# One squaring on the off-diagonal tiles, betas in a pass of their own, key softmax in thirds, twenty pairs per pass

## The reference

```
qkvb = (normed @ W_slow.T).reshape(slen, bsz, H, 5 * D + 2)
q, k, v, rk, rv, beta, rbeta = jnp.split(qkvb, ...)
q, k, rk = softmax(q), softmax(k), softmax(rk)
beta, rbeta = sigmoid(beta), sigmoid(rbeta)
W <- W + beta * outer(v - W k, k)   for each of the 64 rows, z = W q
```

## Time and profile before

| what | us |
|---|---|
| median of 3 runs (20809.05 to 20821.86) | 20810.57 |
| the profiled execution | 20815.45 |
| its span | 20813.7 |
| the delta stage in it, from 6423 to 12034 | 5611 |
| the recurrence behind it, from 12034 to 17085 | 5051 |

### The profile page before, as it was taken

One profiled execution on the slowest core, in us unless ns is written; L12 is line 12 of the kernel. 1 busy time (PEld: TensorE's weight loads), 2 busy tenths in 40 slices (PEclk: granted clock), 3 DMA queues, 4 the chain that ended last, 5 costly groups with the idle time before them and its releaser, 6 DMA issues. The chain is left out here.

```text
span 20813.7 us, 632597 instructions
## 1 busy us (share of the span) xinstructions
PE 14670.6 (70%) x283775; PEld 11976.0 (58%) x283775; DVE 10693.2 (51%) x24317; ACT 6016.6 (29%) x12817; POOL 2224.9 (11%) x1152
## 2 busy tenths in 40 slices
PE   4526777772666989888888966666666665767776
PEld 3414666662445777777777744555544555645554
DVE  6532455555124444444444466666667662445555
ACT  3001244440212444444444411111111111234441
POOL 0066000001460111111111100000000000000001
PEclk9555566665767999999999966777666786877785
DMA  0323200002332111111111122210122215146663
GB/s 21 92 42 70 56 16 13 8 16 77 71 58 61 21 21 20 20 21 20 21 20 21 21 41 40 40 39 17 36 40 41 41 32 153 32 138 183 178 174 76
DMA packets 1836442, 1098.30 MB, mean 53 GB/s; under 512 B 1109402, under 2 KB 1763645, under 8 KB 1816765
## 3 DMA queue, kind: packets, MB, share of 16 engines
q1 hardware_dynamic: 1606323, 999.32, 19.9%
q0 software_dynamic: 227328, 57.19, 1.9%
HBM read 569.43 MB, written 484.53 MB: 51 GB/s over the span
## 5 line engine op out<-in xcount | busy, mean ns | idle before, releaser
L2846 PE MATMUL recur_acc<-recur_U,recur_W 8*32 8x64 f32 (+4 forms) x49152 | 1389.4, 270 | 460.1 <-ACT recur_W L2770 429.3
L2897 DVE TENSOR_TENSOR recur_pr<-recur_K,recur_e 124x64 f32<-124x64 f32 (+60 forms) x1024 | 1285.3, 1255 | 648.3 <-ACT recur_e L2782 493.1
L2846 PEld LDWEIGHTS recur_acc<-recur_U,recur_W 8*32 8x32 f32 (+4 forms) x49152 | 1061.7, 140 | 869.8 <-ACT recur_W L2770 740.2
L2833 PE MATMUL recur_acc<-recur_R,recur_E 128*32 128x64 f32 x62976 | 1202.9, 232 | 187.7 <-issue 177.9
L2902 DVE TENSOR_REDUCE recur_dot<-recur_pr 124x1 f32<-124x64 f32 (+60 forms) x1024 | 1279.2, 1249 | 21.2
L2818 PE MATMUL recur_wT<-const_ident,recur_w 128*128 128x128 f32 (+15 forms) x1536 | 477.8, 373 | 1112.2 <-DVE recur_w L2904 1101.9
L2833 PEld LDWEIGHTS recur_acc<-recur_R,recur_E 128*32 128x32 f32 x62976 | 1073.1, 118 | 288.8 <-issue 230.5
L2770 ACT ACTIVATE recur_W<-recur_wT 128x256 f32<-128x256 f32 (+16 forms) x1024 | 334.8, 327 | 2603.5 <-PE recur_wT L2818 2600.5
L2475 ACT ACTIVATE delta_B0l<-delta_pS 128x512 f32<-128x512 f32 x984 | 531.8, 540 | 1687.4 <-PE delta_pS L2370 1687.4
L2475 ACT ACTIVATE delta_B1l<-delta_pS 128x512 f32<-128x512 f32 x984 | 533.1, 542 | 1407.1 <-PE delta_pS L2370 1407.1
L2818 PEld LDWEIGHTS recur_wT<-const_ident,recur_w 128*128 128x128 f32 (+15 forms) x1536 | 168.2, 143 | 1281.7 <-DVE recur_w L2904 928.2
(11 more groups left out here) (605 smaller groups left out, 34471.9 us busy)
## 6 DMA issues: line engine op xcount, KB each, us to landing
scr<-rel_BD SPq DMA_DIRECT2D x128, 1288.0 KB
rel_sc<-scr SPq DMA_DIRECT2D x128, 861.0 KB
xnT<-ln_xT SPq DMA_DIRECT2D x64, 492.0 KB, 3.0
kr<-delta_QK SPq DMA_DIRECT2D x492, 64.0 KB, 2.3
ur<-delta_Uf SPq DMA_DIRECT2D x492, 64.0 KB, 2.2
zz<-delta_Z SPq DMA_DIRECT2D x492, 64.0 KB, 2.2
recur_K<-kr SPq DMA_DIRECT2D x64, 448.0 KB
recur_H<-zz SPq DMA_DIRECT2D x64, 448.0 KB
```

Of the source, the lines that this page charges most:

```text
L2833: nc.tensor.matmul(acc[a][32 * q:32 * q + 32, 0:FD], E[a][:, EQ * q + 32 * j:EQ * q + 32 * j + 32], R[a][:, m, :], start=(j == 0), stop=False)
L2846: ins = nc.tensor.matmul(acc[a][32 * q:32 * q + 32, 0:FD], W[a][0:8 * k, b, 160 * q + 32 * j:160 * q + 32 * j + 32], U[a][0:8 * k, 2 * (t ...
L2897: V.tensor_tensor(pr[0:cp, 0:n, :], K[a][0:cp, r0:r0 + n, :], e[a][0:cp, None, :].to_broadcast([cp, n, FD]), ALU.mult).then_inc(s_own[a], 1)
```

## The change

- Matrix, transposed matrix and u of a level lie side by side in one buffer (`[128, 4, 3, 64]`). A head's product on the diagonal tiles has 128 moving columns: the transposed matrix and u together, into `pM[k]`. The other square goes from the upper partitions to the lower half of `pS[k]` and from the lower partitions to the upper half, on the two off-diagonal tiles. One semaphore (`s_S`) tells of both; `s_R` is gone.
- ScalarE copies `pS[k]` back in two instructions of 64 partitions each, crossing the halves, then waits until VectorE has read its half of the bank `pM[k]` (`s_dv`), and copies the other half of `pM[k]`.
- The betas of all pairs are computed in a step of their own ahead of the loop: 246 products of 16 columns straight from `X`, 4 sigmoids, 4 square roots. In the loop VectorE copies a pair's betas to a small buffer. 5 projections are left, in slots 0 to 4.
- Maximum, subtraction, exponential and sum are done for each of the three key kinds by itself, in slots 2 to 4, 5 to 7 and 7 to 9 (before: 5, 9 and 12). The scaling stays one instruction.
- A pass of the loop has 20 pairs in place of 6: 6 passes of 20, then the 3 left.

The core of the diff:

```diff
-        pR = [st.ps(f"pR{k}", [128, 8, FD]) for k in range(2)]
-        pS = [st.ps(f"pS{k}", [128, 4, 2, FD]) for k in range(2)]
+        pM = [st.ps(f"pM{k}", [128, 4, 2, FD]) for k in range(2)]
+        pS = [st.ps(f"pS{k}", [128, 8, FD]) for k in range(2)]
...
-        MAX_AT, EXP_AT, SUM_AT = 5, 9, 12
+        MAX_AT, EXP_AT, SUM_AT = 2, 5, 7
...
                         if SQ * G + l:
                             pe.wait_ge(s_ac[k], SQ * G + l)
+                            pe.wait_ge(s_dv[k], SQ * G + l)
+                        more = slice(1, 3) if l < SQ - 1 else slice(2, 3)
                         for a in range(4):
                             for h in HALF:
-                                ins = mm(pS[k][h, a, 0, :], now[h, a, 1, :], now[h, a, 0, :])
-                                if l < SQ - 1:
-                                    ins = mm(pS[k][h, a, 1, :], now[h, a, 0, :], now[h, a, 1, :])
+                                mm(pM[k][h, a, more.start - 1:2, :], now[h, a, 0, :], now[h, a, more, :])
+                            for x, h in enumerate(HALF):
+                                ins = mm(pS[k][HALF[1 - x], a, :], now[h, a, 1, :], now[h, a, 0, :])
                         ins.then_inc(s_S[k], 1)
-                        if SQ * G + l:
-                            pe.wait_ge(s_dv[k], SQ * G + l)
-                        for a in range(4):
-                            for h in HALF:
-                                ins = mm(pR[k][h, a, :], now[h, a, 0, :], u[h, a, :])
-                        ins.then_inc(s_R[k], 1)
...
                             act.wait_ge(s_S[k], SQ * G + l + 1)
-                            m = 2 if l < SQ - 1 else 1
-                            nc.scalar.activation(level(k, G % 2, l + 1)[0][:, :, 0:m, :], pS[k][:, :, 0:m, :], ACT.Copy).then_inc(s_ac[k], 1)
+                            new = level(k, G % 2, l + 1)
+                            for x, h in enumerate(HALF):
+                                ins = nc.scalar.activation(new[h, :, 0, :], pS[k][HALF[1 - x], 0:4, :], ACT.Copy)
+                            if l < SQ - 1:
+                                act.wait_ge(s_dv[k], SQ * G + l + 1)
+                                ins = nc.scalar.activation(new[:, :, 1, :], pM[k][:, :, 0, :], ACT.Copy)
+                            ins.then_inc(s_ac[k], 1)
...
-                        if n == EXP_AT:
-                            act.wait_ge(s_sh, p + 1)
-                            nc.scalar.activation(QK[:, 0:3, :], QK[:, 0:3, :], ACT.Exp).then_inc(s_ex, 1)
+                        if n - EXP_AT in range(3):
+                            j = n - EXP_AT
+                            act.wait_ge(s_sh, 3 * p + j + 1)
+                            nc.scalar.activation(QK[:, j, :], QK[:, j, :], ACT.Exp).then_inc(s_ex, 1)
...
-        NP, US_ = T // 2, 6
+        NP, US_ = T // 2, 20
+        banks = (gp[0][:], gp[1][:], pT[0][:].rearrange("p a d -> p (a d)"), pT[1][:].rearrange("p a d -> p (a d)"))
+        part = lambda n: slice(32 * n, min(32 * n + 32, NP))
+        with st.step() as block:
+            @block.tensor
+            def _(pe):
+                for n in range(4):
+                    for p in range(part(n).start, part(n).stop):
+                        for x, h in enumerate(HALF):
+                            ins = nc.tensor.matmul(banks[n][h, 2 * FH * (p - 32 * n):2 * FH * (p - 32 * n) + 2 * FH], X[:, :, 2 * p + x],
+                                                   W[:, 5 * KW:PROJ], start=True, stop=True)
+                    ins.then_inc(s_g, 1)
...
```

More of the change, by code:

```diff
@@ L2288, in delta_stage @@
         QK = st.sb("QK", [128, 5, KW])
-        sb_ = st.sb("sb", [128, FH, 2])
+        beta = st.sb("beta", [128, T // 2, FH, 2])
+        sb_ = [st.sb(f"sb{q}", [128, FH, 2]) for q in range(2)]
         mx = st.sb("mx", [128, 3 * FH])
@@ L2296, in delta_stage @@
         half_mask = [st.sb(f"hm{what}", [128, FD]) for what in "ULZ"]
-        pair_of = lambda what: (st.sb(f"B{what}", [128, 4, 2, FD]), st.sb(f"U{what}", [128, 4, FD]))
-        first = [[pair_of(f"{k}{g}") for g in range(2)] for k in range(2)]
-        later = [[pair_of(f"{k}l{x}") for x in range(3)] for k in range(2)]
+        first = [[st.sb(f"B{k}{g}", [128, 4, 3, FD]) for g in range(2)] for k in range(2)]
+        later = [[st.sb(f"B{k}l{x}", [128, 4, 3, FD]) for x in range(3)] for k in range(2)]
         level = lambda k, g, l: first[k][g] if l == 0 else later[k][(1, 0, 1, 2)[l - 1]]
@@ L2322, in delta_stage @@
         s_v = st.sem("values_ready")
-        s_R = [st.sem(f"applied{k}") for k in range(2)]
-        s_S = [st.sem(f"squared{k}") for k in range(2)]
+        s_S = [st.sem(f"squared_applied{k}") for k in range(2)]
         s_T = [st.sem(f"tail{k}") for k in range(2)]
@@ L2373, in head @@
                         j, g = divmod(G, 2)
-                        now, u = level(k, g, l)
+                        now = level(k, g, l)
                         if l == 0 and j:
@@ L2507, in _ @@
                     for p in range(preps):
[L2508 to L2509 removed]
+                        for j in range(3):
+                            pool.wait_ge(s_mx, 3 * p + j + 1)
+                            nc.gpsimd.tensor_tensor(third(j), third(j), mx[:, rows_of(j)].unsqueeze(2).to_broadcast([128, FH, FD]), ALU.subtract).then_inc(s_sh, 1)
                         pool.wait_ge(s_sm, p + 1)
[L2511 removed]
+                        nc.gpsimd.tensor_tensor(qk, qk, sm[:].unsqueeze(2).to_broadcast([128, 3 * FH, FD]), ALU.mult).then_inc(s_k, 1)
                 @block.vector
@@ L2644, in _ @@
                         own(nc.gpsimd.tensor_copy(half_mask[m][h, :], full[h, h]))
-        NP, US_ = T // 2, 6
+        NP, US_ = T // 2, 20
[10 more added lines that the diff above has]
+                    ins.then_inc(s_g, 1)
+            @block.scalar
+            def _(act):
+                flat = lambda n: beta[:, part(n)].rearrange("p n h a -> p (n h a)")
+                for n in range(4):
+                    act.wait_ge(s_g, n + 1)
+                    nc.scalar.activation(flat(n), banks[n][:, 0:2 * FH * (part(n).stop - part(n).start)], ACT.Sigmoid).then_inc(s_be, 1)
+                for n in range(4):
+                    act.wait_ge(s_be, n + 1)
+                    nc.scalar.activation(flat(n), flat(n), ACT.Sqrt).then_inc(s_e, 1)
+                act.wait_ge(s_e, 4)
         step_of(0, 0, 1)
```

98 lines of the change are left out of this document (48 added, 50 removed).

## The result

The changed kernel takes 19779.6 us as the median of 4 runs (19740.95 to 19799.73) against 20809.8 us: a ratio of 0.9502, 95% interval 0.949 to 0.9514. A second measurement of both kernels gave 19845.5 against 20879.3 us, 0.9502 again (0.9486 to 0.9518). The forecast was 19820 us with a range of 19500 to 20250.

What follows compares the result with a forecast made beforehand. TensorE's order of work was taken as the bound. From 20810.6 us, 701 for shorter pairs (35.5 against 41.19 us) and 325 for fewer pass ends were subtracted, 35 added for the betas' step: about 19820 us, range 19500 to 20250.

Steps and rivals of the forecast that it cites:

- What bounds it: Delta stage, inside a pair: TensorE's order of work is the bound, 31.2 us of work a pair after the change.
- Heads: TensorE's heads, tiles independent: 0.90 us at levels 0 to 2, 0.46 at level 3, saving 7.9 us a pair.
- tiles in turns: Rival: off-diagonal tiles share strips or keep program order; a head takes 1.36 us, total time 20440 us; chance 14%.
- Copies: ScalarE's copies after a head: 0.38 us each, 0.59 becomes about 1.12 us; ScalarE 23.0 us a pair against 18.4.
- the copies bind: Rival: a ScalarE copy crossing halves costs 0.594 us; a pair takes 38 us, total time 20130 us; chance 14%.
- Waits: TensorE's waits for copies, keys, masks and Z: 4.3 us a pair, bounds 1.7 (as before) to 7.
- The betas' step: One step ahead of the loop with all betas' products and activations: costs 35 us once, from 20 to 150.
- Passes: Ends of a pass, 23.2 us each: 20 become 6, saving 325 us (280 to 350).
- slower: Rival: TensorE's clock falls to 1.2 GHz for a share of the work; at 0.35, total time 21160 us; chance 6%.

Runs made afterwards that it cites:

- the version with the old heads: Changed kernel with the squares back on the diagonal tiles and one ScalarE copy, as before the change: 20321.9 us, 0.9719 of the kernel before; 39.4 us a pair.
- the version with the diagonal square: Changed kernel with the second square on the diagonal tiles too, no copy crossing halves: 20402.7 us, 0.9757 of the kernel before; 40.25 us a pair.
- The late scaling: Changed kernel with reciprocal and scaling of the softmax sums in slot 11 in place of 9: 19781.2 us, 34.8 us a pair.
- the early key: Changed kernel with ScalarE's copy of the second transposed key in slot 17, ahead of the copies of slot 18: 19786.3 us, 34.9 us a pair.
- the three moves together: Changed kernel with scaling in slot 11, second key's copy in slot 17, first two value products in slots 14 and 15: 19657.6 us, 33.9 a pair.
- the whole softmax: Changed kernel with maximum, subtraction, exponential and sum of all three key kinds in one piece again: 20140.9 us, 38.0 us a pair.
- the betas in the loop: Changed kernel with the betas' projection and table loads back in the loop, everything behind one slot later: 20357.8 us, 39.9 us a pair.

## Why the prediction was right, point by point

- **What bounds it**: right. TensorE's work is 35.35 less 3.9 of waits (the rows above and smaller ones, 479 us over 123 pairs without "issue" and the start of the loop), 31.4 us a pair; 31.2 was forecast. Part of this agreement is luck. In the version with the old heads the work is 38.7 us by the same reckoning, so the squares take away 7.3 us where 7.9 was forecast, and the betas some 0.9 where 0.4 was forecast.
- **Heads**: 0.90 us forecast, 0.88 measured. At level 3 0.46 were forecast, and 6844.05 to 6844.57 is 0.52, in a head that starts behind a wait. The tiles run independently; the version with the diagonal square shows that nothing else in the head brings it. The rival "tiles in turns" is refuted by this kernel: narrow and wide records run side by side, and the first narrow records of a head (6840.59) start before records that are issued ahead of them (6840.64 and 6840.69). The Trainium skill, "TensorE: Matmul & The Clock Gate", part 3, has matmuls start and end strictly in program order; over different tiles these rows contradict it for the starts (ends are modelled).
- **Copies**: priced right. The groups of ScalarE, as in the earlier trace rows:

```profile
L2469 ACT ACTIVATE delta_B0l<-delta_pS 64x256 f32<-64x256 f32 x1968 | 743.4, 378 | 868.5 <-PE delta_pS L2369 850.6
...
L2472 ACT ACTIVATE delta_B0l<-delta_pM 128x256 f32<-128x256 f32 x738 | 282.9, 383 | 8.6
...
L2667 ACT ACT_TABLE_LOAD x1 | 1.3, 1283 | 79.6 <-PEq L78 79.6
```

A copy takes 0.378 or 0.383 us where 0.38 was forecast, and one across the halves costs no more than another (0.378 us too in the version with the diagonal square, where nothing crosses). Three table loads are left in the whole stage, one each at L2667, L2670 and L2487 (two in the betas' step and one ahead of the first exponential), where there were three in each pair. The rival "the copies bind" falls with the price.
- **Waits**: 4.3 us a pair forecast, 3.9 measured, but not each where it was put. The stretch of slots 5 to 14 has 1.11 + 0.51 + 0.30 = 1.9 (2.2 forecast), its largest part through the very chain that was followed. The first Gram product waits 1.17 for the keys (0.8 forecast). Masks cost 0.3, Z and the projection together 0.1, where 1.3 was forecast for the three, and a wait for the first copy of a pair (0.3, delta_xc) was not foreseen.
- **The betas' step**: 35 us forecast, 34.8 measured from the stage's first transfer to the first copy (61.4 against 26.6 us). The timeline of it:

```profile
6411.02 15.03 PE L2658 MATMUL delta_gp<-delta_W,delta_X 128*64 128x16 f32 x256 [33.40 <-PEq L78]
...
6425.84 13.87 PE L2658 MATMUL delta_pT<-delta_W,delta_X 128*64 128x16 f32 x236
...
6441.59 2.12 ACT L2670 ACTIVATE delta_beta<-delta_beta 128x512 f32<-128x512 f32 x4
6445.94 0.28 DVE L2540 COPY delta_xc<-delta_X 128x128 f32<-128x128 f32 x1 [67.99 <-PEq L78]
```

The 492 records take 28.7 us (6411.02 to 6439.71): 58 ns each, twice the 29 forecast, at a clock of 0.50 throughout. In return three of the four sigmoids and a table load run beside them, where the forecast had added all eight activations and all three loads. The sum came right with two of its terms off, which is luck.
- **Passes**: 325 us forecast, 331 measured by themselves. In the changed kernel an end costs 55.76 - 35.35 = 20.4 us (19.8 on average of its six), less than before; why was not tested.
- **What the forecast had wrong** is what each edit is worth. It gave the betas 0.4 us of TensorE a pair and counted their table loads as hidden (85 us of waits, "replaced by the waits above"), and it gave the thirds nothing. In the changed kernel the betas' move is worth 4.6 us a pair and the thirds 2.6. The sum survived because it was made for the end state, in which both are gone from ScalarE's path. For the squares alone the same method (work and waits added) gave 37.5 in the expectation above, and 40.8 was measured: it left out that long or close waits also lower the clock. The "slower" rival had this mechanism right, at the wrong place: not the changed kernel pays it, but three versions that lack a part of the change.

What stays open: why whole runs of the same program differ by 0.5% from one measurement to another, mostly in the recurrence and elsewhere; which of betas and thirds brings the 0.8 us of waits with the old heads; and what the betas' product costs TensorE exactly, since the 0.9 us is a difference of two sums. The late scaling, the early key, the three moves together, the whole softmax and the betas in the loop rest on one run each.

## What to carry to other kernels

When the engine that bounds a loop is made faster, price the others in the new order, slot by slot, and not by their share of busy time: here an edit worth 0.4 us a pair alone was worth 4.0 when two small ones had cleared ScalarE's path, and those two were worth 1.8 with the old heads and 5.4 with the new (40.8 less 35.35). Count the clock with the waits: three versions here lost 1.6 to 2.7 us a pair to it by the estimates above. Follow one late instruction through the engines that work in strict order; each of the two waits found that way was cut by about half by moving one line. And products of 64 rows and 64 columns want all four tiles: the same head on two took half as long again.

## What had not been expected of the hardware

- Four 64x64 tiles ran at once without slowing one another, two of them with 128 moving columns at 108 ns a record, two with 64; records started ahead of records of other tiles that were issued before them.
- A standstill of TensorE of 3.8 us inside an otherwise full loop was followed by 3.1 us of work at 1.2 GHz, and three waits of 0.40, 1.41 and 1.18 us close together by 3.5 us of it; 0.51, 1.11 and 0.30 us at the same places did nothing to the clock. The stage's clock was 0.93, 0.95 and 0.99 in these three, and 0.89 with the squares alone. The slow work comes on top of the wait.
- A lone stream of 16-column products of 128 rows, 492 records in 28.7 us, ran at 1.2 GHz from its first record to its last, 58 ns each.
- A subtraction of a third of the columns takes GpSimd 1.04 us, not a third of 2.76.
